# Last group of four images in two halves, and each expert's rows in two transfers

## What is computed

```
h = concat([cls, patches @ W + b] + pos, txt)     # 32 x 114 tokens x 256
n = layernorm(h)
h = h + n + attention(n) @ Wo                     # 16 heads of 64, causal
x = layernorm(h)
gates = softmax(x @ router_w + router_b)          # 8 experts, the best 2 are used
pos = cumsum(mask of the chosen experts) - 1      # place in the expert's buffer
buf[e, pos] = x   where pos < 570                 # capacity 570
out = gelu(buf @ w1 + b1) @ w2 + b2               # 256 -> 1024 -> 256 per expert
h = h + sum over chosen experts of gate * out     # dropped tokens: 0
```

## Time and profile before

| | |
|---|---|
| median of three runs | 906.12 us |
| the profiled execution | 904.56 us |
| its span | 902.6 us |
| mean granted TensorE clock in it | 0.966 |
| busy in the span: TensorE | 837.1 us (93%) |
| VectorE, ScalarE, GpSimd | 559.4, 508.1, 374.4 us |
| chain that ended last, by engine | PE 79%, DVE 11%, issue 4%, ACT 2%, POOL 2%, DMA 2% |

### The profile page before, as it was taken

How to read it: one execution, slowest core, us unless ns; L and a number is a source line. 1 busy time by engine, 2 the same in 40 slices (tenths; PEclk the granted TensorE clock), 3 DMA queues, 4 the chain that set the end, 5 groups by cost and what they waited for, 6 DMA issues and landing times.

```text
span 902.6 us, 19862 instructions
## 1 busy us (share of the span) xinstructions
PE 837.1 (93%) x6897; PEld 755.2 (84%) x6897; DVE 559.4 (62%) x2433; ACT 508.1 (56%) x1686; POOL 374.4 (41%) x677
## 2 busy tenths in 40 slices
PE   4799999999999999999999999998249999999996
PEld 4688898888888889888888878978239999999996
DVE  3567438557665774855856677473337876668771
ACT  3477646656664674665666477372045655556551
POOL 2144324355543643725544465375212324431334
PEclk9799999999999999999999999997559999999999
DMA  8334120021012003102100100100345545544322
GB/s 242 89 96 132 64 66 12 1 65 41 18 35 64 24 1 87 33 2 63 40 10 19 36 18 2 31 11 5 115 117 161 139 97 145 124 113 115 69 28 27
DMA packets 61908, 57.64 MB, mean 64 GB/s; under 512 B 26783, under 2 KB 56651, under 8 KB 61696
## 3 DMA queue, kind: packets, MB, share of 16 engines
q1 hardware_dynamic: 41170, 45.15, 16.5%
q0 software_dynamic: 18944, 9.76, 6.7%
q10 hardware_dynamic: 1696, 1.49, 0.6%
HBM read 34.25 MB, written 21.89 MB: 62 GB/s over the span
## 4 chain that ended last, share of the span: by engine, by line
PE 79%; DVE 11%; issue 4%; ACT 2%; POOL 2%; DMA 2%; POOLq 0%; DVEq 0%
PE bank L359 14%; PE bank L360 13%; PE bank L361 13%; PE score_bank L1168 5%; PE o_bank L1189 5%; PE pT_bank L1177 5%; PE bank L1083 4%; DVE sm L928 2%; PE o_bank L359 2%; PE o_bank L360 2%; PE o_bank L361 2%; PE score_bank L359 2%; PE score_bank L360 2%; PE score_bank L361 2%; PE bank L1144 2%
## 5 line engine op out<-in xcount | busy, mean ns | idle before, releaser
L544 POOL TENSOR_SCALAR pr<-pr,rc 114x114 f32<-114x114 f32 x512 | 180.9, 370 | 294.5 <-DVE rc L962 293.5
L674 ACT ACTIVATE pr<-sm,nb 114x114 f32<-114x114 f32 x512 | 192.3, 383 | 7.7 <-DVE nb L932 7.6
L570 POOL DMA_INDIRECT out_dram<-yout,dest x40 | 74.0, 1850 | 163.4 <-ACT yout L718 161.9
L928 DVE CUSTOM_DVE_ANT_0 sm<-score_bank,mask 114x114 f32<-114x114 f32 x512 | 109.9, 272 | 50.9 <-PE score_bank L1168 50.9
L359 PE MATMUL bank<-xT_hi,wqkv_hi 128*128 128x456 f32 x256 | 105.1, 411 | 2.5 <-DVE qT L748 1.3
L668 ACT ACTIVATE pT<-pT_bank 114x456 f32<-114x456 f32 x128 | 70.6, 551 | 54.7 <-PE pT_bank L1177 54.7
L674 ACT ACTIVATION_READ_ACCUMULATOR pr<-sm,nb 114x1 f32 x512 | 99.2, 194 | 0.0
L360 PE MATMUL bank<-xT_lo,wqkv_hi 128*128 128x456 f32 x256 | 94.4, 369 | 0.0
L361 PE MATMUL bank<-xT_hi,wqkv_lo 128*128 128x456 f32 x256 | 94.3, 368 | 0.0
L526 POOL DMA_INDIRECT slots_dram<-rows,slot x64 | 75.8, 1185 | 35.3 <-DVE slot L907 19.0
L650 ACT ACTIVATE oT_hi<-o_bank 128x228 fp32r<-128x228 f32 x128 | 45.4, 355 | 77.5 <-PE o_bank L1189 67.6
(11 more groups left out here) (198 smaller groups left out, 2214.4 us busy)
## 6 DMA issues: line engine op xcount, KB each, us to landing
stage_a<-in_L_ffn_w_dram SPq DMA_DIRECT2D x8, 1024.0 KB, 4.9
stage_b<-in_L_ffn_w_dram SPq DMA_DIRECT2D x8, 1024.0 KB, 7.1
slots_dram<-fill SPq DMA_DIRECT2D x8, 605.6 KB
xs<-slots_dram SPq DMA_DIRECT2D x8, 605.6 KB
pix<-in_x_dram SPq DMA_DIRECT2D x96, 36.0 KB, 2.2
hraw<-in_txt_dram SPq DMA_DIRECT2D x8, 308.0 KB
out_dram<-h SPq DMA_DIRECT2D x8, 308.0 KB
pix<-pix SPq DMA_DIRECT2D x7, 216.0 KB, 2.5
```

The costliest lines, as they stand in the source:

```text
L544: p = pool.tensor_scalar(pr[:, m % 4, i, :], pr[:, m % 4, i, :], rc[:, m % 4, i:i + 1], 1.0, ALU.mult, ALU.mult)
L570: pool.indirect_dma_start(out, bass.IndirectOffsetOnAxis(ap=dest[e % 2][:, t:t + 1], axis=0), yout[:, t, :], None, compute_op=ALU.add).the ...
L674: a = act.activation(pr[:, N % 4, i, :], sm[:, N % 2, i, :], ACT.Exp, bias=nb[:, N % 2, i:i + 1], scale=SCALE, accum_out=rs[:, N % 4, i:i ...
L928: m = dve.tensor_tensor_reduce(sm[:, N % 2, i, :], score_bank[i % 2][0:T, o:o + T], mask[:, :], 1.0, NEG, ALU.add, ALU.max, mx[:, N % 2, i ...
```

## The change

The last group (7, `LAST`) is treated as two units of two images, `FIRST_HALF` (unit 7) and `SECOND_HALF` (unit 8). Its 16 steps no longer alternate between image pairs: steps 0 to 7 do the eight chunks of images 0 and 1, steps 8 to 15 those of images 2 and 3. Q and K are projected for two images at a time (228 columns), a K and a Q job in each of the steps N = 109 to 124. The output projection has one job per image; those of the first half stand in step 13, its statistics in step 14, its normalised rows in step 15, its transposes, logits, routing parts and counts in the steps 128 to 132 in which the pipeline empties. The routing of group 6 is drawn together (parts 1 and 2 in step 13, 3 and 4 in step 14, its count in step 15, part 5 in step 128). The second half does the same behind the loop. `slot_last` is a second tile for the slot numbers of the halves. In the expert phase each `load_slots` is two transfers with a semaphore each, of three and of two tiles, and `b2b` is loaded behind expert 1's rows.

```diff
-ROUTE_PARTS = (2, 5, 5, 6, 5, 5)
+ROUTE_PARTS = [(2, 5, 5, 6, 5, 5)] * LAST + [(2, 4, 5, 6, 3, 4), (2, 4, 5, 6, 2, 4)]
...
+        ROUTE_LAST = {12: (0,), 13: (1, 2), 14: (3, 4)}
+        FIRST_HALF, SECOND_HALF = LAST, LAST + 1
+        AT_HALF_O, AT_HALF_Y, AT_HALF_L, AT_HALF_C = 13, 0, 1, 4
...
+        def pair_at(m):
+            f, n = divmod(m, PAIRS)
+            return (f, n // 2, 2 * (n % 2)) if f < LAST else (f, n % HP, 2 * (n // HP))
+        def qk_jobs(N):
+            g, n = divmod(N, PAIRS)
+            name, c = ("Q", HP * g + (n + 2) // 2) if n % 2 == 0 else ("K", HP * g + (n + 3) // 2)
+            u = N + 3 - PAIRS * LAST
+            if N >= 0 and c < HP * LAST:
+                return [(name, c)]
+            return [("K", HP * LAST + u), ("Q", HP * LAST + u)] if u in range(PAIRS) else []
...
             def load_slots(e):
-                sp.dma_start(xs[e % 2][:, :, :], slots[...]...).then_inc(slots_in[e % 2], 16)
+                rows_of = slots[e * CAP:(e + 1) * CAP, :].rearrange("(t p) r -> p t r", p=T)
+                for part, (t0, nt) in enumerate(SLOT_PARTS):
+                    sp.dma_start(xs[e % 2][:, t0:t0 + nt, :], rows_of[:, t0:t0 + nt, :]).then_inc(slots_in[e % 2][part], 16)
             load_slots(0)
+            load_slots(1)
             sp.dma_start(b2b[:, :, :], ...).then_inc(b2_in, 16)
-            load_slots(1)
...   (GpSimd, behind the loop)
             for i in range(TOPK * GB):
-                dispatch(G - 2, i)
-            rstd(G - 1, vareps2, rstd2_done, ve2, rstd2)
-            for i in range(TOPK * GB):
-                dispatch(G - 1, i)
+                dispatch(LAST - 1, i)
+            for i in range(TOPK * 2):
+                dispatch(FIRST_HALF, i)
+            rstd(SECOND_HALF, vareps2, rstd2_done, ve2, rstd2, unit_slice(SECOND_HALF))
+            for i in range(TOPK * 2):
+                dispatch(SECOND_HALF, i)
...   (VectorE)
+            def half_statistics(v):
+                for b in unit_images(v):
+                    drain_last_o(b)
+                    dve.wait_ge(dve_drained, drained_by("O", 2 * LAST + b, "d"))
+                    statistics(b, h2, st2, stats2)
+                moments(images_ready(v), unit_images(v), st2, mv2, stats2, moments2)
+                vareps(v, mv2, ve2, moments2, vareps2, unit_slice(v))
...   (VectorE, ahead of the step's masks and reciprocal)
+                if g == G and n == 0:
+                    route(LAST - 1, 5)
+                if g == G and n == AT_HALF_Y + 1:
+                    drain_y(FIRST_HALF)
+                if g == G and n == AT_HALF_L + 1:
+                    route(FIRST_HALF, 0)
...   (VectorE, at the end of the step)
+                if g == LAST and n == AT_HALF_O + 1:
+                    half_statistics(FIRST_HALF)
+                if g == LAST and n == PAIRS - 1:
+                    for b in unit_images(FIRST_HALF):
+                        normalise_rows(FIRST_HALF, b)
+                if g == G and n == AT_HALF_L + 1:
+                    route(FIRST_HALF, 1)
+                    route(FIRST_HALF, 2)
+                if g == G and n == AT_HALF_L + 2:
+                    route(FIRST_HALF, 3)
+                    route(FIRST_HALF, 4)
...   (TensorE, at the end of the step)
+                if g == LAST and n == AT_HALF_O:
+                    for b in unit_images(FIRST_HALF):
+                        project_last_o(b)
+                if g == LAST and n == PAIRS - 1:
+                    count_places(LAST - 1)
+                if g == G and n == AT_HALF_Y:
+                    transpose_tokens("Y", FIRST_HALF, rows[LAST % 2], xn2_done)
+                if g == G and n == AT_HALF_L:
+                    logits(FIRST_HALF)
+                if g == G and n == AT_HALF_C:
+                    count_places(FIRST_HALF)
...   (TensorE, transpose_slots)
-                pe.wait_ge(slots_in[e % 2], 16 * (e // 2 + 1))
                 for i, (k, (t0, nt)) in enumerate(XJOBS):
+                    if k == 0:
+                        pe.wait_ge(slots_in[e % 2][i // KC], 16 * (e // 2 + 1))
```

More of the change, by code:

```diff
@@ L230, in build @@
         b2_in, meta_done = sem("b2_in"), sem("meta_done")
-        slots_in = [sem(f"slots_in{i}") for i in range(2)]
+        slots_in = [[sem(f"slots_in{i}_{part}") for part in range(len(SLOT_PARTS))] for i in range(2)]
         w1_hi_done, w1_lo_done, w2_hi_done, w2_lo_done = (sem(n) for n in ("w1_hi_done", "w1_lo_done", "w2_hi_done", "w2_lo_done"))
@@ L856, in route @@
                 if part == 1:
-                    step(dve.tensor_copy(rows[k % 2][:, :, ID:ID + 1].rearrange("p b o -> p (b o)"), tokid[:, :]))
+                    step(dve.tensor_copy(rows[k % 2][:, im, ID:ID + 1].rearrange("p b o -> p (b o)"), tokid[:, im]))
+                    if k < LAST:
+                        latest()
+                        step(dve.tensor_scalar(tokid[:, :], tokid[:, :], float(GT), None, ALU.add))
+                    dve.wait_ge(lexp_done, v + 1)
+                    step(dve.tensor_reduce(es[:, im], ex[:, im, :], AX.X, ALU.add))
@@ new lines, in route @@
+                    for b in images:
+                        if v < LAST or b + 1 < GB:
+                            latest()
+                            step(dve.tensor_tensor(before[:, b + 1, :], before[:, b, :], chosen[:, b, :], ALU.add))
+                if part == 5:
+                    slots_of = slot if v < LAST else slot_last
+                    dve.wait_ge(filled, job_filled("C", v))
+                    if 0 < v < LAST:
+                        dve.wait_ge(dispatched, 16 * dispatched_by(v - 1))
+                    if v < LAST:
+                        step(dve.tensor_copy(before[:, 0, :], before[:, GB, :]))
+                    dve.tensor_tensor(po_[:, :, im, :], oh[:, :, im, :], job_bank("C", v)[0:T, 0:many * E].rearrange("p (o b e) -> p o b e", o=1, e=E).broadcast_to([T, TOPK, many, E]),
@@ L1137, in project_o, with project_last_o @@
                 m.then_inc(filled, 1)
-            def logits(k):
-                wait_all(pe, drained("Y", KC * k) + drained("Y", KC * k + 1))
-                dst = claim("L", k)
-                for b in range(GB):
+            def project_last_o(b):
+                dst = claim("O", 2 * LAST + b)
+                pe.wait_ge(o_lo, PAIRS * LAST + HP * (b // 2 + 1))
+                for c in range(HP):
+                    m = halves(dst[0:T, 0:D], (oT_hi[:, c, b * T:(b + 1) * T], oT_lo[:, c, b * T:(b + 1) * T]),
+                               (wo_hi[:, c, :], wo_lo[:, c, :]), c == 0, c == HP - 1, pe)
+                m.then_inc(filled, 1)
@@ L1143, in logits @@
+            def logits(v):
+                wait_all(pe, drained("Y", KC * v) + drained("Y", KC * v + 1))
+                dst = claim("L", v)
+                for i, b in enumerate(unit_images(v)):
                     for c in range(KC):
-                        m = pe.matmul(dst[0:T, b * E:(b + 1) * E], x2T[:, c, b * T:(b + 1) * T], router_sb[:, c, :], start=(c == 0), stop=(c == KC - 1))
+                        m = pe.matmul(dst[0:T, i * E:(i + 1) * E], x2T[:, c, b * T:(b + 1) * T], router_sb[:, c, :], start=(c == 0), stop=(c == KC - 1))
```

307 lines of the change are left out of this document (169 added, 138 removed).

## The result

The changed kernel takes 910.06 us (median of 18 runs, 908.64 to 912.46); the kernel before, timed beside it, 906.62 (18 runs, 904.44 to 908.85). The ratio is 1.0037, with a 95% interval of 1.0027 to 1.0046: 3.4 us slower. The forecast was 905.7, no change. The time lies inside the range of 900.5 to 911.5, but the move is real: 18 runs on either side tell 0.1%, not the 0.5% that the prediction allowed itself. The profiled run has a span of 906.2 us against 902.6, at a mean granted clock of 0.964 against 0.966.

The account below looks back on a forecast made before the run. It took TensorE to bound the attention groups, but not the four stretches behind them, where the change acts. Terms: +1.3 to the last scatter, -1.75 for the rows, total -0.4: 905.7 us on the median; 8-in-10 range 900.5 to 911.5.

Parts of the forecast that it names:

- Q and K in halves: Steps 109 to 124: twice as many matmuls at half width plus bank waits in a three-bank ring, +1.0 us in all.
- first half's projection ahead of S: TensorE, step 13: 48 matmuls, 5.7 us, in front of the last scores (S), which move to 611.0.
- last scores to second projection: Run-out from the last scores S: second half's projection starts at S+24.0 against S+12.9, +11.1 us; bounds +6 to +14.
- from there to the slots: From the second projection's end to the slot numbers: one image's work instead of two's, -4.75 us.
- rows in two transfers: Load of the first expert's rows: four transposes left after the second part lands, -1.75 us; bounds -3.3 to +0.3.
- The width: TensorE, Q and K jobs: 228-column matmuls 0.105 us apart, +0.3 us; +2.6 if not under 0.117.
- The claims: Three-bank ring: Q job claims the previous step's K bank, drained late by ScalarE; 0.7 us taken, between 0 and 8.
- Rival B: Steps 109 to 124: Q's claim waits for ScalarE's K drain each step, 5.7 us more, 911 to 914; chance 0.18.
- A cover of 1.5 us: GpSimd: twelve scatters end at 642.4, the second half's `rstd` is wanted at 643.9, so they don't delay it.
- Rival C: GpSimd: the 12 scatters run over `rstd`, +1 to +3 us, 907.5, at most 909; chance 0.10.
- Rival A: Run-out: overlap hides the half's chain, second projection starts at S+18 or 19, 5.5 us sooner, 900.2; chance 0.20.
- Rival D: Load of rows: the split gives nothing (landing in series, or first part hardly sooner), 907.4; chance 0.07.

Follow-up runs that it names:

- e2_halves: The changed kernel with each expert's rows in one transfer again and the bias between them: 909.50 us, ratio 1.0051 to the kernel before.
- e3_order: The kernel before with only the new order of image pairs and the 228-column Q and K jobs in the last group: 908.61 us, ratio 1.0040.
- e6_full: The changed kernel with the run-out reordered (routing, normalisation, transposes, counts later; second `rstd` behind five scatters): 898.85 us, ratio 0.9932 to the kernel before.
- e4_rstd: The changed kernel with the second half's `rstd` ahead of the first half's four scatters: 907.67 us, ratio 1.0016 to the kernel before.
- e5b_count_rstd: The changed kernel with `rstd` ahead of the four scatters and the first half's routing 3, 4 and count behind the loop: 906.74 us, ratio 0.9996.
- e7_swap: The changed kernel with the Q job ahead of the K job in each step: 907.39 us, ratio 1.0006 to the kernel before.
- e8_full_swap: The changed kernel with the reordered run-out of `e6_full` and Q ahead of K: 898.65 us, ratio 0.9915 to the kernel before.
- e1_split: The kernel before with only each expert's rows in two transfers and the second bias behind expert 1's rows: 902.94 us, ratio 0.9979.
- e1b_bias: The kernel before with only the second bias loaded behind expert 1's rows, one transfer an expert: 903.50 us, ratio 0.9998.

## Why the prediction was wrong

Step by step, profile against profile; last scatter's end and first expert matmul are 5.2 and 3.7 us later than before.

| step | sum | measured | |
|---|---|---|---|
| before step 108, nothing changed there | 0 | +1.0 | see what stays open |
| Q and K in halves | +1.0 | +3.3 | 0.3 of it is the late `xn`, not the halves |
| first half's projection ahead of S | +5.7 | +5.3 | |
| last scores to second projection | +11.1 | +10.1 | |
| second projection | -6.0 | -5.4 | |
| from there to the slots | -4.75 | -3.4 | 1.4 of it is `rstd` in the queue |
| four scatters fewer | -5.7 | -5.7 | |
| rows in two transfers | -1.75 | -1.5 | 1.9 in its own experiment |

**The step that failed is the first: "Sum +1.0" for Q and K in halves.** The runs show some +3.0 in its place: +2.9 in the three kernels without the late `xn`, +3.3 with it. Both terms were too small. The width: 0.45 ns a column was carried down from 256 to 228 columns and gave 0.105 us; the matmuls start 0.111 apart, and 192 x 0.1115 less 96 x 0.207 is +1.5, not +0.3. The claims: 0.7 us was taken "since V, O and Y jobs lie between in most steps". Waits were rare, as it says: two of them in 16 steps. But each is 0.5 to 0.8, not 0.2, since the `kT` copy stands behind a `pT` copy and four exponentials. They also stand where the prediction did not look for them: not among steps that have only K and Q, but at the two places where a count or the Y transposes share the ring, so that a K job or the second Y job claims the bank of a K. Rival B named the engine and the copy, but not the claim, which it gave to Q, and its 0.4 a step was under the waits measured; its condition, a wait that repeats each step, did not come true, so it has neither its 5.7 us nor its claim to the result. The kernels with K ahead of Q show +2.9 (`e2_halves`, `e3_order`, `e6_full`) to +3.3 (the changed one, `e4_rstd`, `e5b_count_rstd`) in the stretch, `e7_swap` and `e8_full_swap` without the `kT` waits +2.1 and +2.0, and the time moved with it.

**The second step that failed is "A cover of 1.5 us" on GpSimd.** The train was counted as 12 x 1.43, although show a pause of 2.44 in such a train. With that alone, 2.1 us over the usual 0.3, the cover is gone by the prediction's own numbers; here the pause was 3.74. Of the 1.4 us that `rstd` was late, 1.3 are what this pause is longer than that of the earlier trace rows, so by the measured times a pause of 2.44 would have held it by 0.1 only. Rival C, at 0.10, was this very case: `rstd` right behind a scatter. `e4_rstd`, with `rstd` ahead of the four and a short pause, gets 1.9 back in the times.

The rest stood, and not by luck: the run-out was forecast to a microsecond, with the last reciprocals at S+8.1 and S+12.0 (7.95 and 12.5 in the sum) and both waits for `before` where they were said to be. The run-out came out 1.0 and the first half's projection 0.4 shorter than their terms, which takes back part of the misses. Rival A is refuted: VectorE's order put the half's chain ahead, and the changed kernel's projection came at S+23.0. Rival D is refuted by `e1_split`.

**Where the gain of the halves went.** Behind the start of the second projection 14.5 us are saved (5.4, 3.4 and 5.7); the projection moved ahead of S takes 5.3 and the longer run-out 10.1, together 15.4. That was in the sum. What the sum did not ask is whether the run-out had to grow so: in `e6_full`, which does the same work in another order, it grows by 2.4, so 7.7 us of it were order. `e5b_count_rstd` gives 1.7 of them to the first half's count and the routing that it waits for; the other 6 come from edits that `e6_full` makes together, and no run tells them apart.

**What stays open.** The changed kernel is 0.9 us late between steps 44 and 108, 0.3 at each of three group changes (steps 60, 76 and 92), in code that the change doesn't touch: an `oT_hi` of ScalarE comes some 0.5 later there and the X transposes then wait 0.3 for `xn`. A fourth such wait, at step 108, is in the +3.3 above. `e4_rstd`, `e5b_count_rstd`, `e7_swap` and `e8_full_swap` have it too; `e1_split`, `e1b_bias`, `e2_halves`, `e3_order` and `e6_full` do not. The four with it all ran on one chip (12), and of the five without it four ran on another (10) and one on a third (5); the chip of the changed kernel's profile is not on record. So the edits and the chip are not told apart, and no run here isolates it.

## What to carry to other kernels

Follow the waits of the order as it would be written, and then ask of every instruction ahead of the critical one in its queue whether it must be there: the first half's count, with the routing that it waits for, cost 1.7 us of run-out here only because it stood ahead of a projection that needs neither. With two jobs a step in a ring of three banks, it paid here to put the one with the faster drain first (1.2 us in `e7_swap`). And a train of indirect DMAs on GpSimd is not to be priced by its period alone; what must not wait is safer ahead of it than behind.

## What the runs showed of the hardware that was not expected

The pause in GpSimd's scatters is always behind the third of the train, in all eleven kernels, and it has two lengths: 2.44 us in seven (before, `e1b_bias`, `e1_split`, `e3_order`, `e4_rstd`, `e6_full`, `e8_full_swap`), 3.40 to 3.85 in four (changed, `e2_halves`, `e5b_count_rstd`, `e7_swap`). DMA queues inside the pause, first of the changed kernel (631.97 to 635.71), then of `e4_rstd` (632.57 to 635.01); columns are packets, MB, share of 16 engines:

```profile
q0 software_dynamic: 96, 0.01, 2.8%
q8 instruction: 1, 0.02, 2.2%
q14 instruction: 1, 0.01, 0.8%
```

```profile
q0 software_dynamic: 96, 0.01, 3.5%
```

A packet of an instruction queue lies in each of the four long pauses and in none of the seven short ones. q8 moves 56 packets and 0.92 MB over the whole run, 16 KB each; the Trainium skill, "Runtime: NRT & Kernel Launch", section "Terms", says that an engine's instruction memory is refilled in blocks of 16 KiB, and the packets agree with that size. That this is code loading and that it makes the pause longer is an inference from eleven profiles; no experiment moved it on purpose. What makes the 2.44 us, no row shows: no instruction packet is in them, and the second train of before has no pause at all.

What the granted clock at the start of the last projection costs: the same 48 matmuls took 5.7 us at a granted clock of 1.00 in `e6_full`, behind a run-out of 15.3 us in which TensorE was busy 11.3, and 8.3 us in the changed kernel, where they began at the half level (1.2 of 2.4 GHz) behind one of 23.0 us with 14.0 busy. That the length of the run-out decides this is not shown. `e8_full_swap` began at a lower clock behind nearly the run-out of `e6_full`, and the 96 matmuls of the kernel before began at the half level, those of `e1b_bias` at the full one, both behind 12.9 us.
